# First products by halves of the images, and both halves' averages side by side, in a fused normalise-convolve-rotate kernel

## The reference

```python
def _gn(v, G=32, eps=1e-05):
    g = v.reshape(B_, G, C_ // G, H_, W_)
    m = jnp.mean(g, axis=(2, 3, 4), keepdims=True)
    s = jnp.var(g, axis=(2, 3, 4), keepdims=True)
    return ((g - m) / jnp.sqrt(s + eps)).reshape(v.shape)

x = x + _L0_conv_ref(_gn(x), L0_conv_weight)        # depthwise 5x5, 16 of 25 taps not zero, padding 2
x = x + _L1_conv_ref(_gn(x), L1_conv_rota_matrix)   # out[b,v,h,w] = sum_c R[h,c,v] * gn[b,c,h,w]
```

## Time and profile before

| | |
|---|---|
| median of 3 runs (lowest, highest) | 428.61 us (428.4, 429.36) |
| the profiled execution | 428.04 us |
| its span, first to last instruction | 426.2 us |
| mean granted TensorE clock | 0.985 |
| busy: PE, DVE, ACT, POOL | 407.3, 362.2, 264.4, 242.6 us |
| moved by DMA | 139.83 MB, mean 328 GB/s |

### The profile page before, as it was taken

One profiled execution on the slowest core, in us unless ns is written; L12 is line 12 of the kernel. 1 busy time (PEld: TensorE's weight loads), 2 busy tenths in 40 slices (PEclk: granted clock), 3 DMA queues, 4 the chain that ended last, 5 costly groups with the idle time before them and its releaser, 6 DMA issues.

```text
span 426.2 us, 8616 instructions
## 1 busy us (share of the span) xinstructions
PE 407.3 (96%) x3110; PEld 200.7 (47%) x3110; DVE 362.2 (85%) x691; ACT 264.4 (62%) x513; POOL 242.6 (57%) x312
## 2 busy tenths in 40 slices
PE   7899999999999999999999999999999994999992
PEld 2345555555555555544444445444444541444440
DVE  4899999999999999889998889999887783687872
ACT  2386676667656775696666777666677534477760
POOL 7588675667656765696555676555553153344440
PEclk9999999999999999999999999999999998899997
DMA  8826579599977677977899999999999999999998
GB/s 295 374 58 226 213 221 316 220 334 380 373 250 281 241 272 270 341 255 245 339 360 372 301 384 344 352 391 330 411 361 394 407 377 386 401 427 427 424 425 344
DMA packets 36955, 139.83 MB, mean 328 GB/s; under 512 B 7472, under 2 KB 7600, under 8 KB 24368
## 3 DMA queue, kind: packets, MB, share of 16 engines
q1 hardware_dynamic: 17056, 107.29, 66.5%
q10 hardware_dynamic: 19856, 31.99, 20.8%
HBM read 72.14 MB, written 67.12 MB: 327 GB/s over the span
## 4 chain that ended last, share of the span: by engine, by line
PE 89%; POOL 3%; DMA 2%; issue 2%; DVE 1%; ACT 1%; ACTq 0%; SPq 0%; POOLq 0%
PE ps L743 61%; PE ps L778 26%; POOL area L447 2%; PE ps L784 2%; DMA kept<-x_scratch 1%; DMA norm<-affine 1%; DVE area L652 1%; PE ps L753 1%; PE ps L761 0%; ACT gn L542 0%; POOL gn L470 0%; POOL area L461 0%; ACTq L261 0%; DVE tin L652 0%; ACT std L514 0%
## 5 line engine op out<-in xcount | busy, mean ns | idle before, releaser
L743 PE MATMUL ps<-area 64*64 64x496 f32 (+2 forms) x2560 | 281.6, 586 | 2.4 <-POOL area L447 2.4
L743 PEld LDWEIGHTS ps<-area 64*64 64x64 f32 x2560 | 140.3, 133 | 98.4 <-issue 86.4
L447 POOL TENSOR_TENSOR area<-mask,area 128x325 f32<-128x325 f32 x128 | 132.3, 1056 | 44.3 <-PE ps L743 33.0
L778 PE MATMUL ps<-gn,rot 128*128 128x512 f32 x256 | 117.3, 611 | 6.2 <-ACT gn L542 5.9
L521 ACT ACTIVATE area<-area,affine 128x256 f32<-128x256 f32 x192 | 97.9, 588 | 34.4 <-DVE affine L632 32.5
L534 ACT ACTIVATE area<-ps 64x512 f32<-64x512 f32 x128 | 75.6, 591 | 31.2 <-PE ps L743 28.5
L610 DVE BATCH_NORM_STATS2 stats<-area 128x6 f32<-128x512 f32 x128 | 80.6, 689 | 3.8 <-DMA area<-in_x_dram 3.8
L778 PEld LDWEIGHTS ps<-gn,rot 128*128 128x128 f32 x256 | 48.3, 194 | 72.3 <-issue 60.4
L461 POOL TENSOR_SCALAR area<-area,affine 128x256 f32<-128x256 f32 x62 | 46.1, 752 | 63.3 <-DVE affine L632 63.2
L619 DVE BATCH_NORM_STATS2 stats<-area 128x6 f32<-128x512 f32 x128 | 81.1, 697 | 1.1
L652 DVE TENSOR_TENSOR tin<-ps,tin 128x512 f32<-128x512 f32 x68 | 46.8, 691 | 15.7 <-PE ps L778 15.6
(11 more groups left out here) (26 smaller groups left out, 110.3 us busy)
## 6 DMA issues: line engine op xcount, KB each, us to landing
area<-in_x_dram SPq DMA_DIRECT2D x31, 1024.0 KB, 6.5
x_scratch<-area ACTq DMA_DIRECT2D x29, 1024.0 KB, 7.4
out_dram<-tin SPq DMA_DIRECT2D x17, 1024.0 KB, 8.9
tin<-x_scratch SPq DMA_DIRECT2D x15, 1024.0 KB, 11.4
out_dram<-area SPq DMA_DIRECT2D x10, 1024.0 KB, 13.2
area<-x_scratch SPq DMA_DIRECT2D x7, 1024.0 KB, 11.8
rot<-in_rota_dram SPq DMA_DIRECT2D x4, 1024.0 KB, 9.1
kept<-x_scratch SPq DMA_DIRECT2D x16, 256.0 KB, 10.2
```

What stands on the lines that cost most here:

```text
L447: last = nc.gpsimd.tensor_tensor(taps[k % TRING][:, c * KW:(c + 1) * KW].rearrange("p d (b r) -> p d b r", r=TAPS), mask[:].rearrange("p d ...
L743: last = nc.tensor.matmul(ps[half, bank + c].rearrange("p (j w) -> p j w", j=J)[:, :, outs], taps[k % TRING][rows, (2 * pair + c) * KW + d ...
L778: nc.tensor.matmul(ps[:, rot_bank(m), :], rot[:, n % UNITS * RH + h], gn[n % NRING][:, h], start=True, stop=True).then_inc(rotated, 1)
```

## The change: what it does

1. **Step 0 by halves.** ACT now normalises images 0 to 5 and DVE images 6 and 7 (before: DVE 0 and 1, ACT 2 to 7). A new semaphore, `normed_first`, tells that ACT has done images 0 to 3. The first pair of step 0 goes through a new function, `convolve_images`: five offsets over images 0 to 3, then five over images 4 to 7, each product half as wide (256 columns). The first five wait for `normed_first` alone, the second five for all.
2. **The averages of rounds 1 and 2.** In step 0's first pair the mean of round 1 lies behind the second half's first offset and the spread behind its fourth, both halves together; the mean of round 2 lies behind the fourth offset of the second pair.
3. **DVE's list.** The deviations of step 1 come directly behind its statistics, and the scale of step 1 behind the first two statistics of step 2.
4. **Both halves together.** In every later step the high half's average lies directly behind the low half's, behind offset 0.

```diff
@@ scalar @@
-                for j in range(POOL_J if k else DVE_J, J):
+                for j in range(POOL_J if k else 0, J if k else J - DVE_J):
...
+                    if k == 0 and j == J // 2 - 1:
+                        last.then_inc(normed_first, 1)
                 last.then_inc(normed_act, 1)
@@ vector @@
-            for j in range(DVE_J):
+            for j in range(J - DVE_J, J):
...
             measure(1)
-            measure(2, (0,))
             deviate(1)
-            measure(2, (1, 2, 3))
+            measure(2, (0, 1))
             scale(1)
+            measure(2, (2, 3))
             add_own(0, 0)
@@ tensor @@
+            def convolve_images(js, d):
+                bank = bank_of(0)
+                if d == OFFSETS[0]:
+                    pe.wait_ge(taps_ready, 1)
+                    pe.wait_ge(normed_first, 1)
+                    if js.start > 0:
+                        pe.wait_ge(normed_dve, 1)
+                        pe.wait_ge(normed_act, 1)
+                shift = d - PAD
+                outs, ins = slice(max(0, -shift), W - max(0, shift)), slice(max(0, shift), W + min(0, shift))
+                for rows, half, c in ((low, low, 0), (low, high, 1), (high, low, 1), (high, high, 0)):
+                    last = nc.tensor.matmul(ps[half, bank + c].rearrange("p (j w) -> p j w", j=J)[:, js, outs],
+                                            taps[0][rows, c * KW + d, 0:H], normed[0][rows, c, js, ins],
+                                            start=(d == OFFSETS[0]), stop=(d == OFFSETS[-1]))
+                if js.stop == J and d == OFFSETS[-1]:
+                    last.then_inc(convolved, 1)
...
+            for d in OFFSETS:
+                convolve_images(slice(0, J // 2), d)
             for at, d in enumerate(OFFSETS):
-                convolve(0, 0, d)
-                if at in (2, 3):
-                    average_mean(1, low if at == 2 else high)
-                if at == 4:
-                    average_spread(1, low)
+                convolve_images(slice(J // 2, J), d)
+                if at == 0:
+                    for half in (low, high):
+                        average_mean(1, half)
+                if at == 3:
+                    for half in (low, high):
+                        average_spread(1, half)
             for at, d in enumerate(OFFSETS):
                 convolve(0, 1, d)
-                if at == 0:
-                    average_spread(1, high)
-                if at in (2, 3):
-                    average_mean(2, low if at == 2 else high)
+                if at == 3:
+                    for half in (low, high):
+                        average_mean(2, half)

             for s in range(1, STEPS_ALL):
                 for at, d in enumerate(OFFSETS):
                     convolve(s, 0, d)
-                    if at in (0, 1):
-                        average_spread(s + 1, low if at == 0 else high)
+                    if at == 0:
+                        for half in (low, high):
+                            average_spread(s + 1, half)
                 for at, d in enumerate(OFFSETS):
                     convolve(s, 1, d)
-                    if at in (0, 1):
-                        average_mean(s + 2, low if at == 0 else high)
-                    if at in (3, 4) and s == STEPS_ALL - 1:
-                        average_spread(s + 2, low if at == 3 else high)
+                    if at == 0:
+                        for half in (low, high):
+                            average_mean(s + 2, half)
+                    if at == 3 and s == STEPS_ALL - 1:
+                        for half in (low, high):
+                            average_spread(s + 2, half)
```

More of the change, by code:

```diff
@@ L159, in conv_rotate_kernel @@
         affine_ready = sem("affine_ready")
+        normed_first = sem("normed_first")
         normed_pool = sem("normed_pool")
@@ L730, in convolve @@
                     if pair == 0:
[L731 to L734, removed]
+                        pe.wait_ge(normed_pool, k)
                         pe.wait_ge(normed_act, k + 1)
```

## The result

The changed kernel took 423.87 us (median; 423.3 to 424.82), the kernel before 428.99 beside it: a ratio of 0.988 (0.986 to 0.991), so 5.1 us faster (4.0 to 6.1). The profiled execution took 424.82 (span 422.9), the slowest of its four runs; that of before took 428.04 (span 426.2), less than any of its four runs beside the change (428.40 to 429.71). The two traces are therefore only 3.3 us apart.

The account below looks back on a forecast made before the run. PE, busy 96% of the span, was taken as the bound, with a DMA-bound tail. Start 1.9 plus norms 0.25 gave 2.15 off, so 426.4 (66%, own range 424.9 to 427.6); overall range 424.8 to 428.2.

Parts of the forecast that it names:

- The start: Step 0 by halves and earlier averages: PE begins step 1 at 21.2 in place of 23.13, 1.9 gained.
- rival 3: First pair of step 0: half-wide products show their weight loads, +1.3, giving 427.7; chance 7%.
- Rival 2: At step 1, ACT or DVE is later than PE's own stream: 427.0 (two delays: 427.8); chance 8%.
- The same 0.13 per pair: In 60 further pairs, both averages together cost PE 0.13 per pair as before, +-0.03; period stays 4.33.
- rivals 5 and 6: Side-by-side averages in 60 pairs: 5, all quadrants stop, 435.0 (mild 430.5), 7%; 6, cheaper by 0.06 per pair, 422.9, 5%.
- Rival 4: In the DMA-bound tail, the gain is lost before the end: 428.4; chance 7%.
- "0.25 gained" at the norms: Stall near 180: the earlier root lets the norms be sent 0.25 sooner (0 to 0.6).
- DVE's queue is then what holds it: Behind the earlier root: the scale comes only about 0.25 sooner, because DVE's queue limits it.
- No change in the sum: Averages together over 60 pairs: no change in total time, +-1.8.
- In the steady part nobody waits for that: Steady part: no engine waits for the scale, which comes about 0.25 sooner.
- what PE alone saves after 315 us isn't seen at the end: Tail after 315 us: bound by DMA, so PE's own savings there give nothing at the end.

Follow-up runs that it names:

- experiment 4: Kernel before with the two halves' averages side by side in step 18 alone: 427.93, 0.9 gained, by the ratio 0.7 (0.1 to 1.3).
- experiment 9: Kernel before with ACT's rows of granule 0 moved behind the eviction of step 18's second pair: 427.82, 1.4 gained, by the ratio 1.3.
- Experiments 6 and 7: In the kernel before: 6, only the spread's averages side by side, steps 30 and 31, 427.97 against 429.23; 7, only the mean's, steps 20 to 31, 428.82.
- experiment 5: Changed kernel unedited (424.33), and with 1.7 us of PE work added in step 4 (425.66), step 24 (425.52) or the tail's granules 18 and 19 (424.02).

## Why the prediction was right and wrong

**The start: right.** 1.9 were forecast and 2.06 came, 1.96 without the 0.10 of the input; each mark was within 0.15. Half-wide products hide their loads: the first pair takes 4.43 (12.31 to 16.74), averages included, as against 4.42 before. So rival 3 fell. The rule of the Trainium skill that the prediction set beside it (TensorE: Matmul & The Clock Gate, "Packing small matmuls": a weight load overlaps only products of another row group) would have added 1.1 by its estimate; this trace doesn't agree with it. Rival 2 fell too: ACT was done 0.66 before PE began step 1.

**The same 0.13 per pair: right.** 4.33 stayed 4.33, so rivals 5 and 6 fell. Rival 4 fell as well: the gain wasn't lost before the end.

**"0.25 gained" at the norms: mis-sized.** The change's part was 0.59 on PE. The step that failed was "DVE's queue is then what holds it". In the trace of before DVE has 0.30 to spare ahead of the reciprocals of rounds 8 to 19 (and none ahead of those of rounds 20 to 30); I took this for the whole room. Where only step 18 is changed (experiment 4), DVE does hold it: no wait is left, and the send comes 0.40 earlier against PE. But when the averages come earlier in every step, DVE's list moves forward in every step too, and the send comes 0.59 earlier. What holds it then is ACT: it was idle 0.60 ahead of the root, and in the new trace its row at 169.78 has no idle time left. The range given, 0 to 0.6, held it; the value taken was wrong. At the end of the program the earlier root alone was worth 0.7 (experiment 4), and the eviction ahead of ACT's wait 1.3 (experiment 9), both give or take 0.6.

**"No change in the sum" for the averages, and the seams: a term left out.** Asking only whether a pair's period changes, I didn't ask in what state the pair leaves the quadrants for what follows. The separate averages kept them 0.05 further apart, and each change to the full array paid that: 11 x 0.05 = 0.55. Experiments 6 and 7 show that both pairs of a step must have their averages side by side.

**"In the steady part nobody waits for that": wrong, and the largest miss.** It holds while DVE has statistics to do. In steps 30 and 31 there are none left ahead of the reciprocal; DVE idles 1.03 there, and behind it stand the add, the step's store and the loads of the second layer, at a time when the DMA engines are full. Moving the root (1.3) or only the add (0.9) gains about the same at the end, within wide intervals. The prediction's "what PE alone saves after 315 us isn't seen at the end" fits the stretched tail of experiment 5; the error was to conclude from it that the averages of the last steps change nothing, when they also move what feeds the DMA engines.

Added up, that is 1.96 (start) + 0.59 (stall) + 0.55 (seams) + 1.1 (the middle of 0.9 and 1.3) = 4.2, against 4.4 to 5.2 measured. This is a list of where the gain arose and no proof of its size: the first three terms are PE's, the last is one at the end, and the experiments at the end have intervals of 0.6 to 1 us. In particular an early lead or delay arrives at the end with a factor that the intervals leave between 0.1 and 1.3, and why it should be other than 1 is open. So are what the rest (0.2 to 1.0) is, and which of the transfers in the last steps carries the gain. The profiles don't decide that: PE's wait near 350 us ends anywhere from 355.47 to 356.84 in three profiles of the same changed kernel.

## What to carry to other kernels

When an instruction moves earlier, follow its result to every phase of the program, not only to the steady one: where the next engine's list runs dry the lead passes through, and where a full DMA queue sets the end, it is the issue of transfers that counts, not the busiest engine's time. The idle time ahead of one instruction in one iteration is no cap on what a change gains if the change repeats in every iteration: here 0.40 became 0.59. Where small products are put between large ones on parts of the array, look at the distance between the parts at the next change to the full array. And when two single traces differ by a few tenths, look first for a transfer whose landing varies by as much.

## What the runs showed of the hardware

- A distance between quadrants lives on: a round's four loads take 0.26 in place of 0.21, still four rounds behind the load of the last average (210.94, and the group at 212.62), and the rotation behind them starts 0.05 later.
- Half-wide products (256 columns) in the four quadrants start 0.21 apart and still hide their weight loads of 0.13 each: 40 of them took 4.43 with four averages among them.
- The norms of one step, two transfers of 0.2 KB, took 6.6 to 7.5 us from their issue by ACT until ACT, waiting for them, went on, in all 16 profiles in which it waited for them.
- PE waits near 350 us (5.94 before, 5.29 after) for a granule's normalised rows. In the changed kernel it is idle from 350.73 to 356.01; its granted clock is 1.00 (2.4 GHz) up to 352, 0.50 (1.2 GHz) from 354 to 360 and 1.00 again from 362. What that costs at the end no run shows alone; the 1.72 us that experiment 5 added behind it weren't seen there.
